# Two attention blocks on one core: block 1's tiles between block 0's scores, row maxima in two single PSUM banks, values of two steps together

## The chip, the cores and the metric

The kernel runs on one core of a Trainium2 chip. The metric is the device time of one execution in microseconds (us). Engines are named as in the profile: PE is TensorE's matmuls, PEld its weight loads, DVE is VectorE, ACT is ScalarE, POOL is GpSimd, SP is SyncE, whose queue issues all the transfers.

## The reference

Two blocks follow each other on x of shape (16, 128, 32, 32), float32, so on 16 images with 128 channels and N = 1024 positions each.

```python
# block 0: group norm (32 groups), 4 heads of 32 channels
_x = _group_norm(x, gn_scale, gn_bias)
q, k, v = (_lin_ch(_x, W, b).reshape(B, HEADS, dh, H, W) ...)
scores = jnp.einsum('bhdxy,bhdij->bhxyij', q, k) / sqrt(C)
weights = jax.nn.softmax(scores.reshape(B, HEADS, H, W, H * W), axis=-1)
h = jnp.einsum('bhxyij,bhdij->bhdxy', weights, v).reshape(B, C, H, W)
x = (x + _lin_ch(h, Wp, bp)) / sqrt(2.0)
# block 1: group norm (8 groups), one head of 128 channels
qkv = jnp.einsum('bnc,oc->bno', h_flat, qkv_w) + qkv_b
attn = jax.nn.softmax(jnp.einsum('bnc,bmc->bnm', q, k) / sqrt(C), axis=-1)
out = jnp.einsum('bnc,oc->bno', jnp.einsum('bnm,bmc->bnc', attn, v), proj_w) + proj_b
return out.transpose(0, 2, 1).reshape(B, C, H, W) + x
```

## The kernel before, in words

**Block 0.** For an image the group norm is applied on ScalarE (`norm`, L530), then q, k and v are projected in fp32 (`work`, L812). q and k are split into an fp32r high part (ScalarE, `high`, L540) and an fp32r low part (VectorE, `low`, L653). SP stacks the parts three deep on the partitions (`stack`, L339), so that one fp32r matmul over 97 rows makes a score; row 97 holds the negative row maximum, so exp needs no bias. Scores come transposed, keys on the partitions: a score is a matmul of 512 columns (queries of one half) for one head and one tile of 128 keys. An image has 16 steps (2 halves x 8 key tiles), each with 4 scores, one a head. ScalarE takes each through exp (`exp`, L483) into a slot of `probs`, a ring of 5 blocks; `pv` (L880) multiplies the four heads of a step with v in fp32, 32 columns a head, accumulating over 8 steps in the bank `acc`; GpSimd (`add`, L451) sums the exponentials into `sum0`, two instructions of 128x1024 for a step except the first of a half, 28 an image. At the end of the image TensorE sums over the keys (`sums`), SP sends the sums through `compact`, VectorE takes the reciprocals, SP spreads them through DRAM (`spread_reciprocals`, L385), VectorE scales `mix` (`scale`, L711), and the projection and the residual (`proj`, L853, `residual`, L716) give block 1's input.

The row maxima come earlier and from other matmuls: `masked` holds a copy of q's high part for each head with the other heads' channels zero. 64 matmuls of 128x512 an image (L822) go two by two into one of two pairs of PSUM banks, and one reduce of 128x1024 on VectorE takes each pair (`maxima`, L664). `gather` (L673), a transpose and `shift` (L684) bring the negative maxima into the stack.

**Block 1.** For one image there are 8 query tiles. A tile's scores are 6 fp32r matmuls of 512 columns (`score1`, L914 to L916) into two banks. VectorE reduces 128x1024 (`max1`, L724), ScalarE takes exp with a row sum (`exp1`, L507), TensorE transposes (`turn`, L919), ScalarE evicts (`evict`, L514), TensorE multiplies with v in fp32 (`pv1`, L925, 16 records a tile), ScalarE scales by the reciprocal of the row sum (`oevict`, L521), and after four tiles `out` transposes back and VectorE adds the residual.

**Order of the work.** It is written out by hand. An image's period has two stages: in x (64 gaps) TensorE issues a score of block 0 in each gap, in y (32 gaps) the eight tiles of block 1 of the image before it. Every engine issues in order; tables of pieces (`X_PIECES`, `Y_PIECES` and others) say for each piece in which gap TensorE, ScalarE and VectorE do their part of it. The maxima of the next image stand in gaps of both stages (`MAX_X`, `MAX_Y`). Eight PSUM banks: `acc` 1, `duo` 2, `lone` 1, two pairs of 2. Block 0's scores rotate over `duo` and `lone`, so score n waits for the exp of score n-3. The two pairs serve maxima, q, k, v, means, sums, projection, out; pair 1 and `duo` also serve block 1's tiles; the tiles' outputs go to `lone` and `acc`. In what order they are used is worked out by `pair_uses` (L124), and a piece waits until its pair's last user has given it back.

## Time and profile before

| | us |
|---|---|
| median of 3 runs | 1874.27 (1872.96 to 1874.69) |
| the profiled execution | 1874.44 |
| its span, first to last instruction | 1872.7 |
| PE, PEld busy | 1673.2 (89%), 1050.8 (56%) |
| DVE, ACT, POOL busy | 1057.7 (56%), 1024.9 (55%), 1086.2 (58%) |
| mean granted clock of TensorE | 0.971 |

Busy time of PE counts overlapping records. TensorE's pace is read from the starts of its groups. In the timeline a group is start, length, engine, line, what it writes and reads, shape and count; in brackets stands the idle time before it and what ended it.

### The profile page before, as it was taken

How to read it: one execution, taken by the hardware profiler on the slowest of the kernel's cores; microseconds unless marked ns; L12 is line 12 of the kernel's file. 1: busy time of each engine (PE TensorE's matmuls, PEld its weight loads, DVE VectorE, ACT ScalarE, POOL GpSimd, SP SyncE). 2: the span in 40 equal slices, each digit the busy share in tenths (PEclk: the TensorE clock that was granted, in tenths of full speed). 3: DMA queues.
4: the chain of work that ended last, by engine and by line, in shares of the span. 5: the costliest groups of instructions: out<-in, count | busy, mean ns of one | idle time of the engine just before them, and what ended most of it. 6: DMA issues, size and time to landing. Idle time of an engine off the chain costs nothing.

```text
span 1872.7 us, 24868 instructions
## 1 busy us (share of the span) xinstructions
PE 1673.2 (89%) x9304; PEld 1050.8 (56%) x9304; DVE 1057.7 (56%) x1254; ACT 1024.9 (55%) x1713; POOL 1086.2 (58%) x493
## 2 busy tenths in 40 slices
PE   5888898998989989898998989999898998998878
PEld 3434574745647465564745647475564746555367
DVE  5585646556554655646566554655645565563632
ACT  1535556564655656555564655656555564555644
POOL 1684828477382865828476382856828376493600
PEclk8889999999999999999999999999999999999889
DMA  5031210413122031310313122041311303131000
GB/s 139 24 79 24 66 52 9 96 30 85 41 45 64 18 91 35 79 47 13 84 29 91 35 56 54 17 96 30 79 47 25 73 29 80 35 68 36 1 18 18
DMA packets 52790, 95.41 MB, mean 51 GB/s; under 512 B 27328, under 2 KB 27968, under 8 KB 52672
## 3 DMA queue, kind: packets, MB, share of 16 engines
q1 hardware_dynamic: 52672, 93.83, 20.3%
q8 instruction: 75, 1.23, 0.3%
q14 instruction: 43, 0.35, 0.1%
HBM read 25.89 MB, written 8.65 MB: 18 GB/s over the span
## 4 chain that ended last, share of the span: by engine, by line
PE 45%; issue 27%; POOL 13%; DVE 9%; ACT 5%; DMA 1%; SPq 0%; ACTq 0%; POOLq 0%; DVEq 0%
POOL sum L459 13%; PE acc L939 7%; PE pair L822 7%; DVE halfmax L669 5%; PE lone L939 4%; PE pair L828 4%; PE acc L894 3%; PE duo L922 2%; PE duo L877 2%; ACT probs L498 2%; PE pair L922 2%; PE pair L832 2%; PE pair L850 2%; PE duo L914 1%; PE duo L915 1%
## 5 line engine op out<-in xcount | busy, mean ns | idle before, releaser
L459 POOL TENSOR_TENSOR sum<-sum,probs 128x1024 f32<-128x1024 f32 x437 | 1042.5, 2425 | 527.1 <-PE acc L894 525.0
L669 DVE TENSOR_REDUCE halfmax<-pair 128x2 f32<-128x1024 f32 x512 | 616.9, 1221 | 380.0 <-PE pair L822 378.0
L498 ACT ACTIVATE probs<-duo 128x512 f32<-128x512 f32 x608 | 347.2, 599 | 236.2 <-PE duo L877 198.9
L822 PE MATMUL pair<-k_hi,masked 128*128 128x512 f32 x1024 | 377.2, 452 | 84.4 <-DVE halfmax L669 56.6
L822 PEld LDWEIGHTS pair<-k_hi,masked 128*128 128x128 f32 x1024 | 172.1, 197 | 252.1 <-DVE halfmax L669 102.6
L877 PE MATMUL duo<-q_stack,k_stack 97*128 97x512 f32 x688 | 283.0, 445 | 24.8 <-ACT probs L498 20.5
L894 PE MATMUL acc<-probs,v 128*32 128x512 f32 x1792 | 241.3, 611 | 0.2 <-ACT probs L498 0.2
L498 ACT ACTIVATE probs<-lone 128x512 f32<-128x512 f32 x288 | 173.4, 602 | 101.7 <-PE lone L877 70.4
L877 PEld LDWEIGHTS duo<-q_stack,k_stack 97*128 97x128 f32 x688 | 128.6, 191 | 136.9 <-ACT probs L498 89.7
L939 PEld LDWEIGHTS acc<-v,turned 128*128 128x128 f32 x1280 | 158.9, 192 | 27.2 <-issue 18.8
L939 PE MATMUL acc<-v,turned 128*128 128x128 f32 x1280 | 165.7, 277 | 1.7 <-ACT mixed L527 1.7
L877 PE MATMUL lone<-q_stack,k_stack 97*128 97x512 f32 x336 | 143.7, 428 | 17.4 <-ACT probs L498 17.2
L518 ACT COPY turned<-duo 128x1024 f32<-128x1024 f32 x64 | 64.8, 1013 | 120.9 <-PE duo L922 120.9
L518 ACT COPY turned<-pair 128x1024 f32<-128x1024 f32 x64 | 64.7, 1011 | 117.9 <-PE pair L922 117.9
L443 POOL TENSOR_TENSOR gn<-gn,minus_half 128x1 f32<-128x1 f32 x32 | 18.6, 581 | 184.4 <-DVE gn L645 184.4
L661 DVE SCALAR_TENSOR_TENSOR q_lo<-pair,bq_scaled,q_hi 128x1024 fp32r<-128x1024 f32 x32 | 41.1, 1284 | 115.6 <-ACT q_hi L551 115.6
L877 PEld LDWEIGHTS lone<-q_stack,k_stack 97*128 97x128 f32 x336 | 63.9, 190 | 67.2 <-ACT probs L498 44.4
L726 DVE TENSOR_REDUCE negmax<-pair 128x1 f32<-128x1024 f32 x64 | 78.2, 1222 | 39.2 <-PE pair L916 39.1
L726 DVE TENSOR_REDUCE negmax<-duo 128x1 f32<-128x1024 f32 x64 | 78.2, 1223 | 39.0 <-PE duo L916 37.9
L939 PEld LDWEIGHTS lone<-v,turned 128*128 128x128 f32 x768 | 91.6, 192 | 7.4 <-issue 6.2
L939 PE MATMUL lone<-v,turned 128*128 128x128 f32 x768 | 93.5, 275 | 0.0
L894 PEld LDWEIGHTS acc<-probs,v 128*32 128x32 f32 x1792 | 35.6, 109 | 79.0 <-issue 53.4
(99 smaller groups left out, 2014.8 us busy)
## 6 DMA issues: line engine op xcount, KB each, us to landing
q_stack<-q_hi SPq DMA_DIRECT2D x128, 128.0 KB, 2.4
k_stack<-k_hi SPq DMA_DIRECT2D x128, 128.0 KB, 2.5
xin<-x_dram SPq DMA_DIRECT2D x16, 512.0 KB, 3.7
x<-x_dram SPq DMA_DIRECT2D x16, 512.0 KB, 3.5
masked<-q_hi SPq DMA_DIRECT2D x64, 128.0 KB, 2.4
q_stack<-q_lo SPq DMA_DIRECT2D x64, 128.0 KB, 2.5
k_stack<-k_lo SPq DMA_DIRECT2D x64, 128.0 KB, 2.5
rb<-recip_dram SPq DMA_DIRECT2D x64, 128.0 KB, 2.7
```

Source lines behind the costliest of these rows:

```text
L459: pool.tensor_tensor(total, total, probs[:, ring_slot(i, half, kt), 2 * two:2 * two + 2, :], ALU.add).then_inc(added[two], 1)
L498: act.activation(dst, score_bank(index), ACT.Exp).then_inc(exp_done, 1)
L518: act.copy(turned[:, t % 2, :, :].rearrange("p k n -> p (k n)"), score1_pair(t)[:, :]).then_inc(evicted, 1)
L661: dve.scalar_tensor_tensor(out=lo[:, :], in0=pairs[p][:, :], scalar=bias, in1=hi[:, :].bitcast(F32), op0=ALU.add, op1=ALU.subtract).then_i ...
L669: dve.tensor_reduce(halfmax[:, 2 * two:2 * two + 2, t, half], pairs[p][:, :].rearrange("p (h n) -> p h n", h=2), AX.X, ALU.max).then_inc(p ...
L726: dve.tensor_reduce(negmax[:, t:t + 1], score1_pair(t)[:, :], AX.X, ALU.max, negate=True).then_inc(negmax_done, 1)
L822: mm = pe.matmul(dst[:, halves(n)], masked[:, h, tile(t)], part[2][:, halves(half)], start=True, stop=True)
L828: mm = pe.matmul(dst[:, halves(half)], weight, xh[:, halves(half)], start=True, stop=True)
L877: pe.matmul(score_bank(index), ks[0:SPLIT + 1, h, tile(kt)], qs[0:SPLIT + 1, h, halves(half)], start=True, stop=True).then_inc(score_full, 1)
L894: mm = pe.matmul(acc[head(h), :], v0[:, i % 2, kt, head(h)], src, start=kt == 0, stop=kt == KT - 1, tile_position=(0, DH * h))
L922: mm = pe.transpose(score1_pair(t)[:, tile(kt)], probs1[:, t % 2, tile(kt)], identity)
L939: mm = pe.matmul(out_bank(t), turned[:, t % 2, kt, :], v1[:, kt, :], start=kt == 0, stop=kt == KT - 1)
```

## The change

There is one kind of round in place of the stages x and y: 64 gaps, in each a score of block 0. Block 1's tiles of the image before stand in it, one every 8 gaps from gap 38 of one round to gap 40 of the next. A tile uses the two banks of `scores1` alone, and one copy of `probs1` and of `turned` (in the closing round alone a second set lies in `scores` and `probs`, and tiles stand 4 gaps apart). Banks are now: `scores` 3 (block 0's scores rotate over them), `acc` 1, `scores1` 2, and two single banks for all that the pairs did and for the tiles' outputs (`pv1`). The maxima take a bank each: 64 matmuls and 64 reduces of 128x512 an image, from gap 23 of the round before to gap 10, 11 in 8 gaps, none in gaps 33 to 36 and 42. q, k, v, sums, reciprocals, scale, projection, residual, statistics of block 1 and shift go by halves of 512. `pv` of two steps is issued together in every eighth gap (10, 18, ...). The ring of `probs` has 3 blocks instead of 5. Queries are stacked by halves into three slots and keys into two, so an image has 36 stack transfers instead of 24 (the same bytes), two shift transfers, and twice the sums' and reciprocals' transfers with half the bytes. The last image's adds on VectorE are gone. The head has 32 single maxima of image 0, round 0 the other 32.

```diff
-RING = 5
+RING = 3
-MAX_X = (0, 4, 6, 13, 15, 20, 22, 24, 26, 28, 30, 32, 37, 39, 42, 44, 46, 50, 53, 55, 57, 59, 61, 63)
-MAX_Y = (0, 4, 6, 8, 10, 12, 14, 16)
...
+GAPS = 4 * STEPS
+MAXES = 2 * KT * HEADS
+TILE_GAPS, TILE_FIRST = 8, 38
+def tile_pieces(t, first):
+    return [("score1", (t, 0), 0, first, None, None), ("score1", (t, 1), 0, first + 1, None, None),
+            ("max1", t, 0, None, None, first + 1), ("exp1", t, 0, None, first + 3, None),
+            ("rinv", t, 0, None, None, first + 4), ("turn", t, 0, first + 5, first + 5, None),
+            ("pv1", t, 0, first + 10, first + 11, None)]
+BLOCK1 = [(p[0], p[1], -1) + p[3:] for t in range(KT) for p in tile_pieces(t, TILE_FIRST + TILE_GAPS * t)] + [
+    ("out", 0, -1, GAPS + 11, None, GAPS + 11), ("out", 1, -1, GAPS + 43, None, GAPS + 43)]
+VALUES = [("pv", n, 0, 8 * n + 10, None, None) for n in range(STEPS // 2)]
+MAX_PLACES = (1, 1, 2, 1, 2, 1, 1, 2)
+MAX_FROM = 23
+MAX_NOT = (33, 34, 35, 36, 42)
+MAX_GAPS = [g for g in range(MAX_FROM, 2 * GAPS) if g not in MAX_NOT
+            for _ in range(1 if g == MAX_NOT[0] - 1 else MAX_PLACES[(g - TILE_FIRST) % TILE_GAPS])][:MAXES]
+ALL_MAX = max_pieces(range(MAXES), MAX_GAPS, 1)
+EARLY_MAX = [p for n, p in enumerate(ALL_MAX) if n + 1 < MAXES and MAX_GAPS[n + 1] == MAX_GAPS[n]]
+LATE_MAX = [p for p in ALL_MAX if p not in EARLY_MAX]
+SHIFTS = [("gather", 0, 1, None, None, MAX_HALF), ("shift", 0, 1, MAX_HALF + 1, None, MAX_HALF + 1),
+          ("gather", 1, 1, None, None, MAX_ALL), ("shift", 1, 1, MAX_ALL + 1, None, MAX_ALL + 1)]
+NEXT0 = [
+    ("stats0", 0, 1, None, None, 3), ("mean0", 0, 1, 5, None, 5), ("var0", 0, 1, 7, None, 7),
+    ("affine0", 0, 1, None, None, 11), ("norm0", 0, 1, None, 12, None),
+    ("q0", 0, 1, 17, 17, 18), ("q0", 1, 1, 17, 17, 18), ("k0", 0, 1, 19, 19, 20), ("k0", 1, 1, 19, 19, 20),
+    ("v0", 0, 1, 21, 21, None), ("v0", 1, 1, 21, 21, None),
+]
+CHAIN = [
+    ("save", 0, 0, None, 35, None),
+    ("sums", 0, 0, 44, 44, None), ("recip", 0, 0, None, None, 48), ("scale", 0, 0, None, None, 55),
+    ("proj", 0, 0, 60, None, 60), ("stats1", 0, 0, None, None, 61),
+    ("save", 1, 0, None, GAPS + 3, None),
+    ("sums", 1, 0, GAPS + 6, GAPS + 6, None), ("recip", 1, 0, None, None, GAPS + 9),
+    ("scale", 1, 0, None, None, GAPS + 14), ("proj", 1, 0, GAPS + 15, None, GAPS + 15),
+    ("stats1", 1, 0, None, None, GAPS + 16), ("mean1", 0, 0, GAPS + 22, None, GAPS + 22),
+    ("var1", 0, 0, GAPS + 24, None, GAPS + 24), ("affine1", 0, 0, None, None, GAPS + 28),
+    ("norm1", 0, 0, None, GAPS + 29, None),
+    ("q1", 0, 0, GAPS + 33, GAPS + 33, GAPS + 34), ("q1", 1, 0, GAPS + 33, GAPS + 33, GAPS + 34),
+    ("k1", 0, 0, GAPS + 35, GAPS + 35, GAPS + 36), ("k1", 1, 0, GAPS + 35, GAPS + 35, GAPS + 36),
+    ("v1", 0, 0, GAPS + 42, GAPS + 42, None), ("v1", 1, 0, GAPS + 42, GAPS + 42, None),
+]
+ROUND = folded(EARLY_MAX + VALUES + BLOCK1 + CHAIN + NEXT0 + SHIFTS + LATE_MAX)
...
+def bank_uses(images):
+    back = {VE: dict(all_pieces(VE, images)), SC: dict(all_pieces(SC, images))}
+    uses, counts, last, free = {}, [[0, 0], [0, 0]], [None, None], [(-1, 0), (-1, 0)]
+    for piece, _ in all_pieces(PE, images):
+        if piece[0] in BANKED:
+            b = 0 if free[0] <= free[1] else 1
+            uses[piece] = (b, sum(counts[b]), counts[b][0], counts[b][1], last[b])
+            last[b] = BANKED[piece[0]]
+            free[b] = (back[last[b]][piece], len(uses))
+            counts[b][0 if last[b] == VE else 1] += 1
...
+        scores = ps("scores", [C, 3, HALF])
         acc = ps("acc", [C, HALF])
-        duo = ps("duo", [C, N])
-        lone = ps("lone", [C, HALF])
-        pairs = [None, ps("pair1", [C, N])]
-        pairs[0] = ps("pair0", [C, N])
+        scores1 = ps("scores1", [C, N])
+        banks = [ps(f"bank{b}", [C, HALF]) for b in range(2)]
...
-                    for n, h in enumerate((2 * two, 2 * two + 1)):
-                        mm = pe.matmul(dst[:, halves(n)], masked[:, h, tile(t)], part[2][:, halves(half)], start=True,
-                                       stop=True)
+                    mm = pe.matmul(dst[:, :], masked[:, h, tile(t)], part[2][:, halves(half)], start=True, stop=True)
...
-                dve.tensor_reduce(halfmax[:, 2 * two:2 * two + 2, t, half],
-                                  pairs[p][:, :].rearrange("p (h n) -> p h n", h=2), AX.X,
-                                  ALU.max).then_inc(pair_free[p][VE], 1)
+                dve.tensor_reduce(halfmax[:, h, t, half:half + 1], banks[p][:, :], AX.X,
+                                  ALU.max).then_inc(bank_free[p][VE], 1)
...
+                        if name == "pv":
+                            pv(img, 2 * arg)
+                            pv(img, 2 * arg + 1)
```

An entry of a table names the piece, its argument, the image as an offset from the round's, and the gaps of PE, ACT and DVE. Within a gap the score comes first, then the pieces in the order of `ROUND`: early maxima, values, block 1, chain, next image, shifts, late maxima. `folded` moves entries from gap 64 on into the next round. `bank_uses` gives each piece the bank whose user gives it back first by the gaps of the tables.

## Rows read from the trace of the kernel before

**Rows 1.** The page's head and its busy times, whole execution.

```profile
span 1872.7 us, 24868 instructions
...
PE 1673.2 (89%) x9304; PEld 1050.8 (56%) x9304; DVE 1057.7 (56%) x1254; ACT 1024.9 (55%) x1713; POOL 1086.2 (58%) x493
```

**Rows 2.** Busy time by stage (length, busy by engine, PEclk, DMA share, GB/s).

```profile
0.00:55.90 55.90, 30.68 (x73) 15.36 (x73) 28.87 (x47) 5.76 (x5) 8.56 (x10) 0.77 0.44 117
55.90:149.40 93.50, 84.03 (x358) 41.07 (x358) 65.24 (x65) 44.43 (x74) 67.02 (x30) 0.90 0.24 57
149.40:1704.60 1555.20, 1420.48 (x8065) 899.57 (x8062) 893.12 (x1066) 889.36 (x1490) 960.13 (x433) 0.99 0.21 52
1704.60:1872.70 168.10, 138.03 (x815) 94.81 (x814) 70.50 (x76) 85.33 (x144) 50.50 (x20) 0.93 0.06 18
```

**Rows 3.** Timeline of TensorE, 700 to 745 us.

```profile
700.61 1.95 PE L939 MATMUL lone<-v,turned 128*128 128x128 f32 x16
702.40 0.60 PE L859 MATMUL pair<-consts,mixed 128*128 128x128 f32 x4
...
703.07 0.39 PE L915 MATMUL pair<-k_lo,q_hi 128*128 128x512 f32 x1
703.30 0.39 PE L916 MATMUL pair<-k_hi,q_lo 128*128 128x512 f32 x1
...
704.23 1.03 PE L922 MATMUL duo<-consts,probs 128*128 128x128 f32 x8
705.10 1.06 PE L939 MATMUL acc<-v,turned 128*128 128x128 f32 x8
706.09 1.92 PE L850 MATMUL pair<-sum,ones 128*32 128x512 f32 x16
707.94 1.16 PE L939 MATMUL acc<-v,turned 128*128 128x128 f32 x8
...
741.30 1.98 PE L828 MATMUL pair<-xh,wq_scaled 128*128 128x512 f32 x4
...
743.45 1.06 PE L894 MATMUL acc<-probs,v 128*32 128x512 f32 x8
744.44 0.50 PE L877 MATMUL lone<-q_stack,k_stack 97*128 97x512 f32 x1
744.78 1.88 PE L828 MATMUL pair<-xh,wts 128*128 128x512 f32 x4
```

**Rows 4.** Timeline, 727 to 735 us: reduces on VectorE and maxima around them.

```profile
727.25 1.23 DVE L669 TENSOR_REDUCE halfmax<-pair 128x2 f32<-128x1024 f32 x1 [1.88 <-PE pair L822]
728.39 1.22 DVE L721 TENSOR_TENSOR x<-pair,x 128x1024 f32<-128x1024 f32 x1
...
732.54 1.23 DVE L669 TENSOR_REDUCE halfmax<-pair 128x2 f32<-128x1024 f32 x1 [0.28 <-PE pair L822]
...
733.82 0.73 PE L822 MATMUL pair<-k_hi,masked 128*128 128x512 f32 x2 [0.63 <-DVE halfmax L669]
...
734.59 1.23 DVE L669 TENSOR_REDUCE halfmax<-pair 128x2 f32<-128x1024 f32 x1 [0.39 <-PE pair L822]
```

**Rows 5.** Groups by line and shape (count, busy us, mean ns, idle before); last row: min/median/max.

```profile
L669 DVE TENSOR_REDUCE halfmax<-pair 128x2 f32<-128x1024 f32 x512 | 616.9, 1221 | 380.0 <-PE pair L822 378.0
...
L726 DVE TENSOR_REDUCE negmax<-duo 128x1 f32<-128x1024 f32 x64 | 78.2, 1223 | 39.0 <-PE duo L916 37.9
...
L511 ACT ACTIVATE probs<-duo,negmax 128x1024 f32<-128x1024 f32 x64 | 71.6, 1118 | 4.5 <-DVE negmax L726 4.5
...
L661 DVE SCALAR_TENSOR_TENSOR k_lo<-pair,vecs,k_hi 128x1024 fp32r<-128x1024 f32 x32 | 41.0, 1280 | 46.2 <-ACT k_hi L551 46.2
...
L738 DVE SCALAR_TENSOR_TENSOR x<-pair,proj_bias,x 128x512 f32<-128x512 f32 x32 | 23.8, 745 | 64.5 <-PE pair L859 64.5
...
L714 DVE TENSOR_TENSOR mix<-mix,rb x16: 1225/2770/3056, 161.2 to 1785.0; 128x1024 f32<-128x1024 f32 x16
```

**Rows 6.** Groups of one image's period, 819.5 to 931.6 us.

```profile
L459 POOL TENSOR_TENSOR sum<-sum,probs 128x1024 f32<-128x1024 f32 x28 | 66.5, 2412 | 33.1 <-PE acc L894 33.1
```

**Rows 7.** Timeline of VectorE, 714 to 723 us: reciprocals and scale of one image.

```profile
714.36 0.35 DVE L709 RECIPROCAL compact<-compact 128x32 f32<-128x32 f32 x1 [1.84 <-DMA compact<-rb]
...
722.08 1.50 DVE L714 TENSOR_TENSOR mix<-mix,rb 128x1024 f32<-128x1024 f32 x1 [3.16 <-DMA rb<-recip_dram]
```

More of the change, by code:

```diff
@@ new lines, with rounds_of, pieces_of @@
+LAST_GAPS = LAST_AT[KT - 1, -1] + 12
+PE, SC, VE = 3, 4, 5
+BANKED = {"max": VE, "q0": VE, "k0": VE, "q1": VE, "k1": VE, "v0": SC, "v1": SC, "mean0": VE, "var0": VE, "mean1": VE,
+          "var1": VE, "shift": VE, "sums": SC, "proj": VE, "out": VE, "pv1": SC}
+def rounds_of(images):
+    return [("head", 0, HEAD_GAPS)] + [("round", i, GAPS if i < images else LAST_GAPS) for i in range(images + 1)]
+def pieces_of(kind, i, engine, gap, images):
+    table = HEAD if kind == "head" else ROUND_FIRST if i == 0 else ROUND_LAST if i == images else ROUND
+    return [(p[0], p[1], i + p[2]) for p in table if p[engine] == gap and 0 <= i + p[2] < images]
@@ new lines, in all_pieces @@
+def all_pieces(engine, images):
+    out, before = [], 0
+    for kind, i, gaps in rounds_of(images):
+        out += [(piece, before + gap) for gap in range(gaps) for piece in pieces_of(kind, i, engine, gap, images)]
+        before += gaps
+    return out
+def bank_uses(images):
[8 more added lines that the diff above has]
+            counts[b][0 if last[b] == VE else 1] += 1
@@ new lines, in row_sums @@
+            def row_sums(i, half):
+                piece = ("sums", half, i)
+                p = bank_of(piece)
+                act.wait_ge(bank_full[p], filled(piece))
+                if i:
+                    act.wait_ge(scaled, 2 * i + half - 1)
+                act.copy(rb[:, halves(half)], banks[p][:, :]).then_inc(bank_free[p][SC], 1)
+            act.wait_ge(prep_ve, PREP_VE)
+            for kind, i, gaps in rounds_of(images):
+                for gap in range(gaps):
+                    if kind == "round" and has0(i):
+                        exp(i, gap)
+                    for name, arg, img in pieces_of(kind, i, SC, gap, images):
+                        if name == "turn":
+                            evict(img, arg)
+                        elif name == "pv1":
+                            oevict(img, arg)
+                        elif name == "exp1":
+                            exp1(img, arg)
+                        elif name == "save":
+                            save(img, arg)
+                        elif name in ("norm0", "norm1"):
+                            norm(int(name[-1]), img)
+                        elif name in ("q0", "q1", "k0", "k1"):
+                            high(int(name[-1]), "qk".index(name[0]), arg, img)
+                        elif name in ("v0", "v1"):
+                            value(int(name[-1]), arg, img)
+                        elif name == "sums":
+                            row_sums(img, arg)
@@ L807, in take @@
-                if after_tiles and p == 1:
-                    pe.wait_ge(evicted, after_tiles)
-                return pairs[p], pair_full[p]
-            def work(piece, tiles):
-                name, arg, i = piece
-                dst, full = take(piece, tiles)
+                    pe.wait_ge(bank_free[p][last], by_ve if last == VE else by_sc)
+                dst = banks[p]
                 b = int(name[-1]) if name[-1] in "01" else 0
                 if name == "max":
-                    t, half, two = arg // 4, arg // 2 % 2, arg % 2
+                    t, half, h = arg // 8, arg // 4 % 2, arg % 4
```

910 lines of the change are left out of this document (386 added, 524 removed), and 12 rows, old and new, of tables (HEAD, HEAD_PIECES, X_PIECES, Y_LAST_PIECES).

## The prediction

> **What bounds the kernel now.** I read the page's head first, then busy time by stage, then TensorE's timeline, then the other engines' rows. TensorE is busy 89% of the span, no other engine over 58% [rows 1]; ahead of the first score stand 55.9 us, then 93.5 us for image 0's scores, 1555.2 us for fourteen like rounds (111.1 each, clock 0.99) and 168.1 us of tail [rows 2]. TensorE's rows are pipelined and overlap, so I count from start to start [rows 3]: a 512-column fp32r matmul 0.23 (703.07 to 703.30); a tile's eight transposes 0.87 (704.23 to 705.10); its sixteen value records 1.79 (700.61 to 702.40); values of one step of block 0 0.99, and the score behind them 0.34 instead of 0.23 (743.45, 744.44, 744.78), so each change to or from fp32 with 32 columns costs 0.1; two groups of row sums together 1.85 (706.09 to 707.94), so the second of two such groups costs only 0.86. A q with one score is 2.15 (741.30 to 743.45), so 1.72 for q itself.
>
> With these, an image of before needs: 64 scores, 64 maxima and 48 tile scores, 176 x 0.232 = 40.8; turns 8 x 0.87 = 7.0; tile values 8 x 1.79 = 14.3; block 0's values 16 x 1.2 = 19.2; q and k 6.9, v 3.6, projection 1.7, sums 2.0, out, means, shift 2.1. Sum 97.6 against 111.1: some 13.5 us per round are waits of TensorE. The change has to lower those, or the round gets no shorter.
>
> **The change, part by part.**
> *Values of two steps together:* one entry and exit saved per pair and the overlap of 1.85 against 2 x 0.99: 0.99+0.86+0.2 = 2.05 instead of 2.4, eight pairs: -2.8. Bound from the other side: nothing saved. I take -2.8, from the sums row.
> *Halves of q, k, v, projection, out:* same matmuls. Sums by halves 2 x 1.2 instead of 2.0: +0.4; a second shift +0.2. New need of TensorE: 95.4.
> *Single banks for the maxima:* 64 reduces of 512 in place of 32 of 1024. The trace has none. Lower bound half of 1.22, 0.61; by the shape that exists both ways (low parts, 1.28 for 1024, 0.745 for 512 [rows 5]) 512 elements save 0.53: 0.69, which I take; upper bound the 0.745 itself. VectorE then has about 70 us of work in a round (64 x 0.69, 8 x 1.22, 8 x 0.745, and 10 of small ones), so it is no bound. But the loop through one bank is: a matmul of 0.40 ends and the reduce starts 0.04 later, the matmul that waited starts 0.05 after the reduce [rows 4]; so a bank is back 0.43+0.69+0.05 = 1.17 after its matmul started. Before, a pair took 0.23+0.43+1.22+0.05 = 1.93 but carried two matmuls, and ScalarE's output tiles stood in other banks. Now pv1, out, sums, q, k, v share the two.
> *Tiles between scores:* every 8 gaps hold 8 scores, a tile (6 scores, turn, values), a value pair, and 11 maxima. Time 0 at the first gap, from the rows above:
> gaps 1, 2: score, three tile scores, maximum 1 (0.93); score, three tile scores (last at 1.86), maximum 2 at 2.09. VectorE's list has the tile's reduce of 1024 before maximum 2: it runs 2.29 to 3.51 [rows 5], maximum 2's reduce 3.43 to 4.12 (back to back an op starts 0.09 before the end of the last, as at 728.39 [rows 4]).
> gap 3: score, maximum 3, and the last tile's values take maximum 2's bank: could start 2.78, start at 4.17. **Wait 1.39.** They end 5.87; maximum 4.
> gap 4: score, maximum 5 in the bank of maximum 4: 6.42 becomes 7.04. **Wait 0.62.**
> gap 5: score, maximum 6, value pair, maximum 7; gap 6: turn, maximum 8 (exp of the tile, 1.12 [rows 5], is ready); gap 7: maximum 9; gap 8: maxima 10, 11: **waits 0.16 and 0.37.**
> So 2.5 us per full cycle. I went through all 64 gaps of a round so, by the order of the lists. Gaps 38 to 45: 1.39+0.62, sums behind out 0.5, maxima behind the sums copy 0.35: 2.9. 46 to 53: 2.0, and shift between maxima 1.3: 3.3. 54 to 61: 2.0, scale ahead of a maximum 1.1, maxima behind the projection 0.8: 3.9. 62 to 5: 2.3, statistics (1.5 on VectorE) ahead of a maximum and mean between two maxima 1.8: 4.1. 6 to 13: 1.15+0.62, and the second shift, which TensorE reaches 1.6 before out's add, affine and gather are through: 3.4. 14 to 22: 0.6. 23 to 29: 3.0. 30 to 37: q behind a maximum 0.6, maxima behind k's low parts 1.2: 1.8. Sum of waits 23.0; round 95.4+23.0 = **118.4 us** against 111.1.
> *Scale:* its row is 1.2 at least, 2.77 in the median [rows 5]; for halves I took 0.7 to 1.5. The Trainium skill ("SBUF — State Buffer", section "SBUF: two separate sides") has VectorE with two SBUF inputs and GpSimd lock each other out for a whole instruction; the spread of that row agrees. By it a half would still wait out an add: 0.9 more per round, 1981 in all.
> *Queues and ring:* GpSimd's adds are 28 x 2.41 = 66.5 per image [rows 6]; ring 3 needs an add within some 5 gaps (9 us) and gets it in 4.8 to 7: nothing in full rounds. Sync's queue issues 36 stack transfers instead of 24, all behind gap 18 and due a round later: nothing, with the rest of the round as cover; without it one more set of 12, some 8 us. The reciprocals: recip stands 8.3 us behind the sums' start, scale 7.4 behind recip [rows 7]; the new places leave 7.5 and 7 or more, so at most 1 us, taken as 0.
> *The ends:* head: no statistics of image 1 (-2), one shift transfer for four (-2), single reduces (+2): 54. Round 0: the adds bound it: they start at gap 10 (17 us), the second half starts at gap 42 (52), and the exp of gap 60 needs eight adds of it (19): 71, and 4 to its end: 75. Round 1 lacks four tiles (21) and 3 of waits: 94.4. Rounds 2 to 15: 14 x 118.4 = 1657.6. Tail: sums of the last half at 7, reciprocals to 20, projection, norm, q, k to 38, eight tiles x 4.05 = 32, last values, out, store 14: 84 to 86, I take 85.
> Sum 54+75+94.4+1657.6+85 = 1966; what lies around the span is 1874.4-1872.7 = 1.7 (the profiled execution is 0.2 over the median shown): **1968**. It turns on the round: 1.7+190+15 x P for a round P (the span of before is met at P = 112.2).
>
> **Rivals.**
> (a) *TensorE's waits are fewer* (faster). Place: the irregular stretches. A wait makes the next one shorter, and of the 23 us I may count neighbours twice; if only the regular waits of the six tile cycles stay, 13.7 minus a little, P = 108: 1812. It decides from waits under 16.8 per round. For it: before has only 13.5. Against: each is a row's loop with nothing between; the cycle was followed through. 0.13.
> (b) *Even*, waits of 16 to 17.5: 1874. 0.04.
> (c) *The pairing saves nothing* (the change doesn't do that part): P = 121.2: 2010. 0.08.
> (d) *The clock.* It stood at 0.99 with 13 us of waits and at 0.90 to 0.93 in the sparser ends [rows 2]. If the rounds went to 0.92, TensorE's need is 95.4/0.93: P about 125, 2065. 0.05. The Trainium skill ("TensorE: Matmul & The Clock Gate", section "A second HAM failure mode: psum-queue depth-cycling") tells of small idles between groups that cycle through banks and bring the clock down; the 0.99 beside 13 us of waits per round speaks against; by the rule it would be (d)'s 2065.
> Forecast: 0.70.
>
> **Numbers.** The reduce's bounds move about a dozen waits a round each by its error once or twice: 0.61 gives P = 116, 0.745 gives 120: 1930 to 1990; with my error in the irregular waits, 3 us a round each way, 1900 to 2010. To hold 8 in 10 the range takes in (b), part of (a) and (c): 1860 to 2020. Faster by over 0.2% (about what a measurement here can tell from no change) 0.13, within 0.04, slower 0.83.
>
> **What would show it.** Score 0 of one round to the next 118 apart; reduces of 128x512 at 0.69; tile values waiting 1.4 for a maximum's reduce, that behind the tile's own reduce; the second of two maxima in one bank 0.6 late; no GpSimd wait within full rounds; value pairs 1.85 long; granted clock over 0.97. Wrong: a round under 112, or waits of TensorE mostly for exps or adds.

## The result and the profile after

| | before | after |
|---|---|---|
| median | 1874.5 us (4 runs) | 2067.2 us (4 runs, 2065.3 to 2068.1) |
| ratio to before | | 1.103, interval 1.101 to 1.105 |
| span of the profiled execution | 1872.7 | 2063.2 |

The change makes the kernel 10% slower. The sign was forecast, with 0.83; the size was not: 1968 was said, 1860 to 2020 as the range, and the measured time lies 47 us above its upper end.

The page's head, busy times and chain of the kernel after:

```profile
span 2063.2 us, 26122 instructions
...
PE 1733.4 (84%) x9319; PEld 1070.5 (52%) x9319; DVE 1128.9 (55%) x1897; ACT 1061.1 (51%) x1825; POOL 1103.3 (53%) x504
...
PE 65%; DVE 24%; issue 5%; ACT 3%; DMA 2%; SPq 1%; POOL 0%; ACTq 0%; DVEq 0%; POOLq 0%
PE bank L912 12%; DVE halfmax L708 12%; PE bank L879 12%; PE acc L838 11%; PE scores L825 7%; PE scores L863 5%; DVE negmax L750 4%; PE bank L887 3%; PE scores L855 3%; PE scores L857 3%; PE bank L883 3%; PE scores L856 3%; DVE mix L737 2%; PE bank L901 2%; DVE k_lo L699 2%
```

TensorE's share falls from 89% [rows 1] to 84%, and no other engine is fuller: nobody is the bound. The chain says what is: it goes to and fro between TensorE and VectorE. VectorE has 24% of it with 55% busy, and half of that is the reduces of the maxima (L708).

By stage (head, round 0, round 1, thirteen rounds, round 15, tail; columns as in [rows 2]):

```profile
0.00:58.30 58.30, 33.35 (x68) 15.26 (x68) 31.64 (x56) 6.44 (x8) 11.42 (x9) 0.79 0.41 112
58.30:149.00 90.70, 80.05 (x297) 35.85 (x297) 62.13 (x100) 42.68 (x73) 64.92 (x29) 0.86 0.21 50
149.00:255.80 106.80, 89.23 (x416) 47.32 (x415) 64.27 (x108) 54.36 (x93) 68.62 (x33) 0.92 0.19 45
255.80:1883.90 1628.10, 1378.00 (x7568) 860.48 (x7567) 910.07 (x1535) 859.73 (x1482) 887.68 (x404) 0.98 0.19 47
1883.90:1971.60 87.70, 80.49 (x503) 52.06 (x502) 32.91 (x56) 59.27 (x106) 60.09 (x27) 1.00 0.06 19
1971.60:2063.20 91.60, 72.26 (x475) 59.56 (x473) 27.87 (x46) 38.60 (x64) 10.58 (x6) 0.93 0.05 15
```

The thirteen full rounds take 1628.1/13 = 125.2 us each where 118.4 was said. TensorE has no matmul under way for 250.1 of the 1628.1 us, 19.2 a round. The waits view of the whole execution (us in total, times, longest):

```profile
PEld bank L879 <- DVE halfmax L708: 221.5, 330, 4.3
...
PEld bank L912 <- DVE halfmax L708: 150.8, 82, 3.9
...
PE bank L912 <- DVE halfmax L708: 115.3, 69, 3.5
...
PE bank L879 <- DVE halfmax L708: 82.8, 166, 4.0
```

Two things wait for a maximum's reduce: the next maximum's matmul (L879) and the values of block 1's tile (L912). Weight loads and matmuls overlap, so the first and last number are not to be added; of the matmuls alone it is 115.3 + 82.8 = 198.1 us. The groups by form give the reduce and the scale:

```profile
L708 DVE TENSOR_REDUCE halfmax<-bank 128x1 f32<-128x512 f32 x1024 | 679.1, 686 | 446.4 <-PE bank L879 444.1
...
L737 DVE TENSOR_TENSOR mix<-mix,rb 128x512 f32<-128x512 f32 x32 | 57.0, 1780 | 4.6 <-DMA rb<-recip_dram 4.5
```

The reduce of 128x512 takes 0.686 us, as said (0.69), 56% of the 1.221 of the double one [rows 5]. The scale of a half takes 1.78 in the mean, where 0.7 to 1.5 was counted.

**One tile, as it repeats.** Timeline of the kernel after, a tile's last scores, its reduce and its neighbour's values:

```profile
1131.22 0.39 PE L857 MATMUL scores<-k_hi,q_lo 128*128 128x512 f32 x1
...
1131.45 0.39 PE L879 MATMUL bank<-k_hi,masked 128*128 128x512 f32 x1
...
1131.65 1.23 DVE L750 TENSOR_REDUCE negmax<-scores 128x1 f32<-128x1024 f32 x1 [0.21 <-PE scores L857]
...
1132.79 1.28 DVE L708 TENSOR_REDUCE halfmax<-bank 128x1 f32<-128x512 f32 x2
...
1133.53 2.05 PE L912 MATMUL bank<-v,turned 128*128 128x128 f32 x16 [1.22 <-DVE halfmax L708]
...
1135.34 0.48 PE L879 MATMUL bank<-k_hi,masked 128*128 128x512 f32 x1
...
1135.85 0.69 DVE L708 TENSOR_REDUCE halfmax<-bank 128x1 f32<-128x512 f32 x1 [1.78 <-PE bank L879]
...
1136.60 0.50 PE L879 MATMUL bank<-k_hi,masked 128*128 128x512 f32 x1 [0.55 <-DVE halfmax L708]
```

The maximum of 1131.45 could be reduced at 1131.88. VectorE's list has the tile's reduce of 1024 first (1131.65 to 1132.88), so its bank is back at 1133.48, and the values of the tile before, which take that bank, stand at the head of TensorE's queue with everything behind them. That is the wait forecast at 1.39; the gaps of the steady rounds give 1.49. The next pair of maxima in one bank was put at 0.62 and is 0.82: the fp32r matmul right behind fp32 groups lasts 0.48 to 0.50 instead of 0.40, so the reduce behind it starts later.

**Where the scale stands.** The same kernel, one gap of each round:

```profile
1111.81 4.71 POOL L509 TENSOR_TENSOR sum<-sum,probs 128x1024 f32<-128x1024 f32 x2
...
1113.39 0.39 PE L879 MATMUL bank<-k_hi,masked 128*128 128x512 f32 x1
...
1113.59 1.22 DVE L750 TENSOR_REDUCE negmax<-scores 128x1 f32<-128x1024 f32 x1 [0.24 <-PE scores L857]
...
1114.73 2.33 DVE L737 TENSOR_TENSOR mix<-mix,rb 128x512 f32<-128x512 f32 x1
1116.99 1.27 DVE L708 TENSOR_REDUCE halfmax<-bank 128x1 f32<-128x512 f32 x2
1117.72 2.58 PEld L912 LDWEIGHTS bank<-v,turned 128*128 128x128 f32 x16 [3.91 <-DVE halfmax L708]
1117.72 2.67 PE L912 MATMUL bank<-v,turned 128*128 128x128 f32 x15 [3.47 <-DVE halfmax L708]
...
1120.25 0.77 PE L879 MATMUL bank<-k_hi,masked 128*128 128x512 f32 x1
```

And by stretch, the wait and what follows it (columns as in [rows 2], the granted clock third from the end):

```profile
1115.00:1117.70 2.70, 0.00 (x0) 0.00 (x0) 2.70 (x3) 0.00 (x0) 1.52 (x1) 1.00 0.00 0
...
1118.80:1122.20 3.40, 3.04 (x12) 2.32 (x12) 0.69 (x1) 0.71 (x2) 0.04 (x1) 0.51 0.00 0
```

In this gap the tile's reduce and then the scale stand ahead of the maximum's reduce. The scale lasts 2.33 us: it ends at 1117.06, half a microsecond after GpSimd's add (1111.81 + 4.71 = 1116.52). Where no add runs the same multiply takes 0.69 (the last one of this trace, at 1993.26). It takes 0.67 where it comes just at the change from one add to the next, and then the add behind it lasts 2.89 instead of 2.4 (e1's timeline below, at 1087.16). So most of the 2.33 is waiting for the add. The Trainium skill ("SBUF — State Buffer", section "SBUF: two separate sides") calls the port pair shared by VectorE with two SBUF inputs and GpSimd "an exclusive lock, not a bandwidth split"; this trace agrees, 2.33 beside an add against 0.69 without.

**What the long wait does to TensorE's clock.** Gap 56 has a median of 7.56 us, 5.07 more than its 2.49 in e8, the shortest of all runs. Not all of that is waiting. After the 3.47 us without a matmul TensorE's granted clock falls from 1.00 to 0.5, its level of 1.2 GHz, and the values and the maximum behind them take 2.88 us (all sixteen records) and 0.77 instead of 2.05 and 0.48. It does so in gap 56 of eleven of the thirteen full rounds (7.56 us in the mean); in the two without a fall the gap takes 6.18 and 6.22. So the wait itself is 3.7 us, and 1.4 are TensorE working at half its clock. Gap 6 shows the same: 3.79 us in the mean of nine rounds with a fall there, 2.36 in the four without. Ahead of it stand only short waits (in this round 0.73 and 0.30 us, behind maxima's reduces, at 1017.32 and 1018.60). Together the falls leave TensorE at 0.5 for 5.3 us of a full round and cost about 2.1 us of it (my sum of the gaps: (9 x 1.43 + 11 x 1.36)/13).

### The profile page after: what moved, and what is told of

Read it like the earlier page. It is cut to its first block, busy times and chain, and to the rows that moved or that the text cites. A ratio compares the mean times of both kernels' runs of the same rounds, so it can differ in the third digit from the quotient of the medians.

```text
span 2063.2 us, 26122 instructions
## 1 busy us (share of the span) xinstructions
PE 1733.4 (84%) x9319; PEld 1070.5 (52%) x9319; DVE 1128.9 (55%) x1897; ACT 1061.1 (51%) x1825; POOL 1103.3 (53%) x504
## 4 chain that ended last, share of the span: by engine, by line
PE 65%; DVE 24%; issue 5%; ACT 3%; DMA 2%; SPq 1%; POOL 0%; ACTq 0%; DVEq 0%; POOLq 0%
PE bank L912 12%; DVE halfmax L708 12%; PE bank L879 12%; PE acc L838 11%; PE scores L825 7%; PE scores L863 5%; DVE negmax L750 4%; PE bank L887 3%; PE scores L855 3%; PE scores L857 3%; PE bank L883 3%; PE scores L856 3%; DVE mix L737 2%; PE bank L901 2%; DVE k_lo L699 2%
## 5 line engine op out<-in xcount | busy, mean ns | idle before, releaser
L708 DVE TENSOR_REDUCE halfmax<-bank 128x1 f32<-128x512 f32 x1024 | 679.1, 686 | 446.4 <-PE bank L879 444.1
L544 ACT ACTIVATE probs<-scores 128x512 f32<-128x512 f32 x896 | 523.4, 601 | 649.7 <-PE scores L825 647.2
L879 PE MATMUL bank<-k_hi,masked 128*128 128x512 f32 x1024 | 486.4, 480 | 119.1 <-DVE halfmax L708 82.8
L825 PE MATMUL scores<-q_stack,k_stack 97*128 97x512 f32 x1024 | 445.1, 445 | 2.2 <-DMA q_stack<-neg 2.2
L879 PEld LDWEIGHTS bank<-k_hi,masked 128*128 128x128 f32 x1024 | 199.6, 195 | 386.5 <-DVE halfmax L708 221.5
L912 PE MATMUL bank<-v,turned 128*128 128x128 f32 x1952 | 261.5, 290 | 116.6 <-DVE halfmax L708 115.3
L912 PEld LDWEIGHTS bank<-v,turned 128*128 128x128 f32 x1952 | 244.3, 202 | 156.5 <-DVE halfmax L708 150.8
L825 PEld LDWEIGHTS scores<-q_stack,k_stack 97*128 97x128 f32 x1024 | 196.9, 194 | 71.3 <-issue 28.7
L750 DVE TENSOR_REDUCE negmax<-scores 128x1 f32<-128x1024 f32 x128 | 156.7, 1225 | 77.3 <-PE scores L857 77.3
L557 ACT ACTIVATE probs<-scores,negmax 128x1024 f32<-128x1024 f32 x128 | 143.0, 1117 | 3.4 <-DVE negmax L750 3.4
L855 PE MATMUL scores<-k_hi,q_hi 128*128 128x512 f32 x256 | 105.2, 411 | 4.4 <-DVE k_lo L699 3.2
```

Of the source, the lines that this page charges most:

```text
L544: act.activation(dst, score_bank(i, index), ACT.Exp).then_inc(exp_done, 1)
L708: dve.tensor_reduce(halfmax[:, h, t, half:half + 1], banks[p][:, :], AX.X, ALU.max).then_inc(bank_free[p][VE], 1)
L750: dve.tensor_reduce(negmax[:, t:t + 1], score1_pair(j, t), AX.X, ALU.max, negate=True).then_inc(negmax_done, 1)
L825: pe.matmul(score_bank(i, index), ks[0:SPLIT + 1, i % 2, h, tile(kt)], qs[0:SPLIT + 1, q_half(i, half), h, :], start=True, stop=True).then ...
L855: pe.matmul(dst, q_hi[:, tile(t)], k_hi[:, halves(half)], start=True, stop=False)
L879: mm = pe.matmul(dst[:, :], masked[:, h, tile(t)], part[2][:, halves(half)], start=True, stop=True)
```

## The experiments

Theory A, from the two timelines: a round's TensorE work is what was counted (95.4), and the rest are waits of TensorE at the head of its queue for a reduce that stands late in VectorE's list; the two single banks are what ties the two queues together. Rival B: the round is longer for a reason that the gaps don't show one by one (adds, exps, the smaller ring, a slower TensorE). Rival C: it is the other parts of the change, the pairs of values or the single kind of round.

Times and ratios below are medians of 4 runs (e5 and e6 of 2, e12 of 10) against the kernel before on the same chip. A full round is the mean over rounds 2 to 14, from score 0 of one to score 0 of the next; its "waits" are each gap's median length less the TensorE work counted for it, 95.4 a round. So they hold what TensorE loses at the lower clock too, and they can't confirm the count.

| run | us | ratio [interval] | full round | waits in it | at clock 0.5 |
|---|---|---|---|---|---|
| after | 2067.2 | 1.103 [1.101, 1.105] | 125.2 | 29.8 | 5.3 |
| e1 tile's reduce last | 1941.5 | 1.037 [1.035, 1.039] | 116.3 | 20.5 | 0.3 |
| e2 first scale on GpSimd | 2004.7 | 1.070 [1.069, 1.072] | 121.7 | 26 | 2.1 |
| e3 values one by one | 2077.4 | 1.109 [1.107, 1.110] | 125.9 | | 3.2 |
| e4 three banks | 1805.6 | 0.963 [0.962, 0.965] | 107.4 | 12.4 | 1.8 |
| e8 e1 + e2 + e4 | 1745.6 | 0.933 [0.931, 0.934] | 103.6 | 7.8 | 0.0 |
| e10 e8, pieces a gap later | 1750.0 | 0.934 [0.933, 0.936] | 103.6 | 7.9 | 0.0 |
| e11 e8, values one by one | 1768.9 | 0.944 [0.942, 0.946] | 105.3 | 9.7, or 6.9 of a work of 98.2 | 0.0 |

The last column is how long TensorE's granted clock stands at 0.5 in a full round, in us. In the kernel before it is 2.4.

**e1: the order of VectorE's list alone.**

```diff
-                    for name, arg, img in pieces_of(kind, i, VE, gap, images):
+                    for name, arg, img in sorted(pieces_of(kind, i, VE, gap, images), key=lambda p: p[0] == "max1"):
```

> Edit of the changed kernel: within a gap VectorE does the tile's own reduce of 1024 last, behind the maxima of that gap. Theory A (TensorE waits because the two single banks come back only through VectorE's queue): the tile values' wait of 1.49 us, six times a round, shrinks to about 0.5; 6 us a round less, round 125.2 to 119, total about 1980 us. Theory B (tiles between scores cost by themselves, through ScalarE or the changes of type): no change, 2067 us.

Measured: 1941.5. The same place of a tile in e1's timeline, and a scale further on:

```profile
1060.70 0.39 PE L879 MATMUL bank<-k_hi,masked 128*128 128x512 f32 x1
...
1061.13 0.69 DVE L708 TENSOR_REDUCE halfmax<-bank 128x1 f32<-128x512 f32 x1 [0.44 <-PE bank L879]
...
1061.73 1.22 DVE L750 TENSOR_REDUCE negmax<-scores 128x1 f32<-128x1024 f32 x1
1061.87 1.86 PEld L912 LDWEIGHTS bank<-v,turned 128*128 128x128 f32 x16 [0.75 <-DVE halfmax L708]
1061.87 2.05 PE L912 MATMUL bank<-v,turned 128*128 128x128 f32 x16 [0.32 <-DVE halfmax L708]
...
1087.16 0.67 DVE L737 TENSOR_TENSOR mix<-mix,rb 128x512 f32<-128x512 f32 x1
```

The maximum is reduced at once, the values wait 0.32 instead of 1.22 (0.58 instead of 1.49 by the gaps), and in gap 56 it is 1.44 instead of 5.07. Nothing else was changed, no instruction added or removed: 126 us of the 193 that the change costs come from the place of one reduce among its neighbours. A full round is 8.9 shorter, not the 6 expected, because two things follow from the shorter wait. The scale in gap 55 takes 1.50 us instead of 2.33 (it starts 0.9 later in GpSimd's add, and again ends 0.55 after it), and the clock, which fell 20 times in the thirteen full rounds, falls once, some 2 us of the 8.9. So the slower TensorE that B names is there, but as a consequence of these waits; for the rest B is out for this part.

**e2: the first half's scale on GpSimd**, behind its add of that gap instead of beside it.

```diff
+                        pool.wait_ge(rb_loaded, 16 * HEADS * (2 * i + 1))
+                        pool.wait_ge(saved, 2 * i + 1)
+                        pool.tensor_tensor(mix[:, halves(0)], mix[:, halves(0)], rb[:, halves(0)],
+                                           ALU.mult).then_inc(scaled, 1)
...
-                            scale(arg, img)
+                            if arg:
+                                scale(arg, img)
```

> Edit of the changed kernel: the scale of an image's first half is done on GpSimd, behind its add 21 and the forming of x1, instead of on VectorE between two reduces in gap 55. Theory A: the wait of 5.07 us in gap 56 falls to the 1.49 us of the other tiles, 3.6 us a round less, total about 2015 us. Theory B: 2067 us. If GpSimd's place is too late, the projection in gap 60 waits and eats the gain.

Measured: 2004.7; gap 56 waits 1.49, as a regular tile. GpSimd does it in 1.30 us (20.8 us for 16, group L527) and TensorE waits 0.3 us for it in the whole run. So one instruction of a half, at its place, costs the kernel 62 us, 3.5 a round, where the sum had held 1.1 for it. About 2.2 of the 3.5 are its wait (3.7 in gap 56 without a fall, less the 1.49 of a regular tile), most of the rest is the lower clock behind it, which no longer comes in gap 56.

**e3: pairs of values undone.**

```diff
-VALUES = [("pv", n, 0, 8 * n + 10, None, None) for n in range(STEPS // 2)]
+VALUES = [("pv", n, 0, 4 * n + 6, None, None) for n in range(STEPS)]
...
-                            pv(img, 2 * arg)
-                            pv(img, 2 * arg + 1)
+                            pv(img, arg)
```

> Edit of the changed kernel: block 0's values one step at a time again, every four gaps, three gaps behind the step's last score, as the pair stands behind its second step. Pairing as computed (2.05 us for two instead of 2.4): 2.8 us a round more, total about 2109 us. Rival (a pair of 2 us blocks TensorE and costs more than it saves): total under 2067 us. If the extra 0.35 us lie in waits for VectorE's banks anyway: about 2067 to 2085 us.

Measured: 2077.4, so 10 us for all the pairs, 0.7 a round (0.9 by the gaps' medians) in place of 2.8. C is out for the pairs: they are not what costs, and they hardly help here. That what a pair saves of TensorE's work is spent in the next wait for a bank fits, but no run shows it by itself. The single kind of round is no cause either: e5 and e8 below keep it.

**e4: three single banks, two banks of scores** in place of two and three, so that score n waits for the exp of score n-2.

```diff
-        scores = ps("scores", [C, 3, HALF])
+        scores = ps("scores", [C, 2, HALF])
...
-        banks = [ps(f"bank{b}", [C, HALF]) for b in range(2)]
+        banks = [ps(f"bank{b}", [C, HALF]) for b in range(3)]
...
-            b = 0 if free[0] <= free[1] else 1
+            b = min(range(3), key=lambda k: free[k])
```

> Edit of the changed kernel: three single banks for maxima and the rest, two instead of three for block 0's scores; nothing else. Theory A: of the 29.8 us of waits in a round the tile values', the second maximum's and the double maxima's go; 8 to 12 us stay (scale, statistics, q and k), round 104 to 108, total 1770 to 1830 us. Rival (TensorE then waits for exps, with two score banks): over 1950 us. Theory B: 2067 us or more.

Measured: 1805.6, inside theory A's range, 262 us less, and faster than before. Waits fall from 29.8 to 12.4 a round. The bank that the scores lose is hardly missed: in the thirteen full rounds a score's weight load waits 23.6 us in all for an exp, 1.8 a round, and no wait of its matmul for one is among the larger. Its waits view has the first line of the one above at 123.9, and none of the tile's values behind a reduce among its larger ones:

```profile
PEld bank L879 <- DVE halfmax L708: 123.9, 228, 5.9
...
PE bank L879 <- DVE halfmax L708: 49.2, 51, 5.4
```

**e5 and e6: the maxima left out**, in the kernel after and in the one before. Both compute only those of the row maxima that the order of the waits needs (5 of 64 in e5, 3 of 32 double ones in e6) and start `halfmax` at zero; everything else is done.

```diff
-    return [(p[0], p[1], i + p[2]) for p in table if p[engine] == gap and 0 <= i + p[2] < images]
+    return [(p[0], p[1], i + p[2]) for p in table if p[engine] == gap and 0 <= i + p[2] < images
+            and (p[0] != "max" or p[1] in (0, 30, 31, 62, 63))]
```

> Edit of the changed kernel: of the 64 maxima of an image only numbers 0, 30, 31, 62 and 63 are made, the others' places hold zero, so the shift of the scores is another; all else stays. Theory A (the waits are those behind the maxima's reduces): the need falls by 59 x 0.23 = 13.7 to 81.8 us a round and the waits from 29.8 to 4 or 6 us, round 86 to 88, total 1490 to 1530 us. Theory B (tiles between scores cost by themselves): the waits stay near 20 us, total over 1700 us.

> Edit of the kernel before: of the 32 pairs of maxima only numbers 0, 15 and 31 are made, the others' places hold zero; all else stays. It gives what the maxima cost in the old order: their need is 29 x 0.46 = 13.3 us an image; if they also bear half of its 13.5 us of waits, about 91 us an image, total 1540 us; if they bear none, 98 us, 1655 us. Both theories agree here; the difference to the changed kernel without maxima is what the new order is worth by itself (theory A: the new order is the shorter one by 30 to 60 us, theory B: the longer one).

Measured: e5 1551.6 (0.829), rounds of 90.0; e6 1702.0 (0.909), 101.4 from image to image. By stage, e5's full rounds and e6's images:

```profile
203.30:1373.90 1170.60, 1089.56 (x6801) 710.86 (x6800) 425.16 (x767) 843.43 (x1483) 890.39 (x404) 1.00 0.26 65
```

```profile
122.20:1440.00 1317.80, 1204.99 (x6759) 714.87 (x6756) 385.91 (x622) 817.75 (x1387) 889.24 (x403) 0.95 0.23 57
```

Both missed what was expected, and together they say more than either: without maxima the new order is 150 us **shorter** than the old one, with them 193 longer. The maxima cost the old order 1874 - 1702 = 172 us and the new one 2067 - 1552 = 515, which is 32 an image. Of these 59 x 0.232 = 13.7 are the matmuls; the other 18.5 are waits that only the maxima bring, with the lower clock behind some of them. Taking them out of the old order saves less than their own matmuls (172/16 = 10.8 an image, where 29 x 0.46 = 13.3 are matmuls). Its waits view shows one reason, more waits for exps:

```profile
PEld duo L879 <- ACT probs L499: 184.5, 254, 2.6
```

against 89.7 us for that pair with the maxima there. A second reason is the clock, 0.95 in e6's stage line and 1.00 in e5's: TensorE stands at 0.5 for 10.2 us of every image of e6, 2.4 in the kernel before. Half of the difference, up to 3.9 us an image or some 60 us in all, can be the lower clock; the two reasons are not separated, and up to that much of the 150 us between e5 and e6 can be the clock's. My reading is that in the old order the maxima filled holes between exps, and that in the new one, with the tiles spread out, few such holes are left (8 us a round in e5), so that the maxima make their own.

**e7: pairs of values in the old order.**

```diff
-                            if (n, h) == (2, 0) or (n >= 2 and h == 2):
-                                pv(i, n - 1 - (h == 0))
+                            if n >= 2 and n % 2 == 0 and h == 2:
+                                pv(i, n - 2)
+                                pv(i, n - 1)
...
+                        pv(i, STEPS - 2)
                         pv(i, STEPS - 1)
```

> Edit of the kernel before: block 0's values two steps together, all else as it was; this part of the change alone. If TensorE's need sets the old stages: 16 x 2.8 = 45 us less, 1829 us. If what TensorE saves is lost in waits for exps and adds: 1850 to 1874 us. Over 1874 us if the pair of 2 us starves ScalarE.

Measured: 1933.2 (1.033 [1.030, 1.035]): the edit that was to shorten TensorE's work costs 59 us, 4.1 an image. From score 0 the scores run with those of before within 1.9 us up to the middle of the image; by score 43 they are 3.3 us late, and the first add behind `rstd` starts at 60.1 instead of 57.4. TensorE's clock falls to 0.5 26 times in thirteen images instead of 9. In the kernel before an image with a fall takes 112.1 and one without 110.7, so by that price the clock can be some 1.9 of the 4.1.

**e9: the same with the first and last step of each half alone**, six pairs an image.

> Edit: the kernel before, values of two steps issued together as in e7, but the first step of each half (0 and 8) and the last of each half (7, 15) alone and where they stood; six pairs an image instead of eight. In e7 the first add of the second half, which waits for the values of step 8, started 60.1 us after score 0 instead of 57.4, and the image took 116 instead of 112.1 (e7: 1933). If that late value is what made e7 slower: the add of the second half is back at 57.4, and the six pairs save at most 6 x 0.35 = 2.1 us an image: 1840 to 1875. If two steps together stall ScalarE or the score banks by themselves: six eighths of e7's loss stay, 1905 to 1925.

Measured: 1918.4 (1.024 [1.023, 1.026]), add at 60.0. A late first value is not the cause. The timeline shows another:

```profile
664.25 0.73 PE L822 MATMUL pair<-k_hi,masked 128*128 128x512 f32 x2
...
665.16 1.92 PE L894 MATMUL acc<-probs,v 128*32 128x512 f32 x16
...
667.01 0.38 PE L838 MATMUL pair<-gn,consts 128*128 128x1 f32 x2
...
667.43 0.16 DVE L645 TENSOR_SCALAR gn<-pair 128x1 f32<-128x1 f32 x1 [1.18 <-PE pair L838]
...
667.67 0.55 POOL L443 TENSOR_TENSOR gn<-gn,minus_half 128x1 f32<-128x1 f32 x1 [7.59 <-DVE gn L645]
...
668.19 4.70 POOL L459 TENSOR_TENSOR sum<-sum,probs 128x1024 f32<-128x1024 f32 x2
...
670.73 0.60 ACT L498 ACTIVATE probs<-lone 128x512 f32<-128x512 f32 x1 [2.35 <-POOL sum L459]
...
671.37 0.50 PE L877 MATMUL lone<-q_stack,k_stack 97*128 97x512 f32 x1 [2.00 <-ACT probs L498]
```

An image takes 114.0 against 111.0 before. The only one of the thirteen in which the clock doesn't fall takes 113.2, against 110.7 for those of the kernel before, so 2.5 of the 3.0 are there at the full clock.

Read from below: a score waits for an exp, the exp for a slot of the ring, the slot for GpSimd's add, the add for `rstd` ahead of it in GpSimd's list (idle 7.59 us), `rstd` for VectorE, VectorE for a small matmul of TensorE, and that stands behind the pair of values. A loop through four engines, and the pair lengthens it.

**e12: `rstd` four adds later in GpSimd's list**, else e9.

```diff
-                    if n == 14 and has0(i + 2):
+                    if n == 18 and has0(i + 2):
```

> Edit: e9 (before with six value pairs an image, 1918 us) and GpSimd computes the next image's rstd behind add 18 of an image instead of add 14. Seen in e9's trace: GpSimd's add 15 stands behind rstd, rstd behind VectorE's var0, var0 behind a matmul that TensorE issues after a value pair of 1.92 us; the adds start 2.6 us later than before (60.0 instead of 57.4 after score 0), an exp waits 2.35 us for one of them, and a score 2.00 for that exp. If this detour of GpSimd is where the pairs lose their time, the 2.6 to 3.3 us an image that are lost behind gap 44 come back and more: 1865 to 1885. If the time goes where TensorE's long pair leaves ScalarE without scores, rstd changes little: 1905 to 1920.

Measured: 1872.7 (1.000 [0.999, 1.001], 10 runs), inside the first theory's range: 46 us from one instruction moved. Its images take 110.6 without a fall of the clock and 112.1 with one, as those of before, so 2.6 of what came back is at the full clock. The add behind add 14 starts at 51.8 instead of 60.0, and the waits view has

```profile
ACT probs L498 <- POOL sum L459: 7.3, 2, 7.1
```

against 70.5 in e9 and 65.8 before. It is not the whole story of the pairs. ScalarE's waits for scores (the lines `ACT probs` behind `duo` and `lone`) are 269.5 us before, 314.5 in e9 and 337.6 in e12, so six pairs in the old order give nothing even then. Whether the later `rstd` without any pairs beats the kernel before was not tried.

**e8: the three edits together** (e1, e2, e4).

> The changed kernel with three single banks, the tile's reduce last in its gap, and the first half's scale on GpSimd. With three banks 12.4 us of waits are left in a round of 107.9, 4.4 of them in gaps 56 and 58 around the scale. Theory A: these go, the tile's order adds 0 to 0.5, round 104, total 1745 to 1760 us. If GpSimd's place for the scale is too late: the projection's gap takes the wait over, 1790 to 1806 us.

Measured: 1745.6, inside the first theory's range and 6.7% less than before: the best version here. Its full rounds (13 of them), and its chain:

```profile
223.90:1570.80 1346.90, 1296.45 (x7567) 851.07 (x7567) 870.67 (x1522) 856.97 (x1482) 902.82 (x417) 1.00 0.23 57
```

```profile
PE 75%; DVE 13%; issue 4%; ACT 4%; DMA 2%; SPq 1%; POOL 1%; ACTq 0%; DVEq 0%; POOLq 0%
```

**e10: e8 with `mean0`, `var0` and the second shift one gap later**, where its largest waits were left.

```diff
-    ... ("mean0", 0, 1, 5, None, 5), ("var0", 0, 1, 7, None, 7),
+    ... ("mean0", 0, 1, 6, None, 6), ("var0", 0, 1, 8, None, 8),
...
-          ("gather", 1, 1, None, None, MAX_ALL), ("shift", 1, 1, MAX_ALL + 1, None, MAX_ALL + 1)]
+          ("gather", 1, 1, None, None, MAX_ALL), ("shift", 1, 1, MAX_ALL + 2, None, MAX_ALL + 2)]
```

> Edit: e8 (1746) with mean0 and var0 one gap later (6, 8) and the second shift one gap later (13), since the two largest waits left in its round stand there (gap 12 1.29 us, gap 5 1.14). If each wait is only a static order by which TensorE reaches a piece before VectorE has got to it, both fall to 0.3 or so: 1.5 to 1.8 us a round, 1718 to 1728. If what a wait gives back is mostly taken by the next (the banks are the bound), 0 to 0.5 a round: 1738 to 1750.

Measured: 1750.0, no gain, as the second theory had it. Gap 5's wait of 1.14 became 0.63, 0.34 and 0.53 in gaps 5, 6 and 8; gap 12's 1.29 became 1.18 in gap 13. A likely reason is that TensorE reaches a moved piece just as early relative to its neighbours on VectorE, since both lists moved together.

**e11: e8 with the values one by one**, e3's edit.

> Edit: e8 (1746) with the values of one step in every fourth gap instead of two in every eighth. In e3, with 30 us of waits in a round, undoing the pairs cost 0.9 us a round, where I had counted 2.8 of TensorE's need. If the 2.8 were right and e3's waits swallowed the rest, then here, with 8 us of waits, it costs 2 to 2.8 a round: 1776 to 1791. If the pairs save less of TensorE than I counted, about 0.9 a round: 1755 to 1765.

Measured: 1768.9, between the two ranges and 23 us more than e8. A round takes 105.3 against 103.6 (105.2 against 103.2 by the gaps' medians). So the pairs are worth 1.7 to 1.9 of the 2.8 where few waits are left, and 0.7 to 0.9 where many are.

## Why the prediction was right and wrong

Its span of 1966 against the 2063.2 measured, by its own terms: head 54 became 58.3 (+4), round 0 75 became 90.7 (+16), round 1 94.4 became 106.8 (+12), thirteen full rounds +89, round 15 118.4 became 87.7 (-31), the tail 85 became 91.6 (+7). Sum +97.

**What held.** The single-bank reduce is 0.686 for 0.69. TensorE's need, 95.4, was counted from single rows and is not measured by itself; it agrees with e8, whose 103.6 us a round leave 8.2 above it, and with e5 (90.0, its need 81.8). The mechanism is the one named: values of a tile behind a maximum's reduce behind the tile's own reduce (1.49 for 1.39), the second maximum in one bank (0.82 for 0.62). The ring of three, the 36 transfers and the reciprocals cost nothing in full rounds: what waits there is named by the waits view, and it is mostly the reduces.

**The step that failed: the waits of a round, 23.0, where its gaps leave 29.8 above the count.** About 27.2 of these are waits. The other 2.6 are TensorE at the lower clock in a usual round, for which the sum held nothing; rival (d) had the clock at a chance of 0.05. By stretch, said and measured: gaps 38 to 45 2.9, 3.3; 46 to 53 3.3, 3.7; **54 to 61 3.9, 6.8**; 62 to 5 4.1, 4.2; 6 to 13 3.4, 4.8; 14 to 22 0.6, 0.7; 23 to 29 3.0, 4.0; 30 to 37 1.8, 2.3. None came out smaller. The clock's falls stand in two of them: 1.4 of the 6.8 in gap 56, and 1.3 of the 4.8 in gap 6, nearly all that 6 to 13 has above what was said.
- The largest piece is "0.7 to 1.5" for the scale of a half. The row had shown 2.77 in the median for the whole [rows 5], and the sum took the lower half of it; measured 2.33 beside an add, which made gap 56 5.07 (3.7 of waiting, 1.4 of lower clock) instead of the cycle's 1.39 and what the scale was given. The lock of the Trainium skill ("SBUF — State Buffer", section "SBUF: two separate sides"), which the prediction had kept apart at 0.9 a round, held; the scale's whole price was 3.5 (e2). It stands, with the tile's reduce, ahead of the reduce that frees a bank, and the clock falls behind so long a wait.
- The loop through one bank was counted with the plain matmul of 0.40. Behind fp32 groups it is 0.50, so 1.27 in place of 1.17, six or more times a round.
- Irregular places with several small VectorE pieces between two maxima (gaps 5, 24, 29, 37) were each 0.3 to 0.6 short.

**Round 0.** "The adds bound it: 71, and 4 to its end" gave 75. Without maxima that is right (e5: 73.7). With them the banks bind this round too: 90.7, and 81.7 with three banks (e4). The first half's scale is as large a part of it: it takes 4.01 us in this round (at 132.72, across two adds), and with it on GpSimd the round is 83.4 (e2). Round 1 likewise, 77.0 in e5 against 106.8.

**Round 15** was counted as a full round in "rounds 2 to 15: 14 x 118.4". It has no next image, so no maxima, q, k, v of one. That error of 31 us went the other way and hid a quarter of the rest; with its measured length the same sum gives 1937.

**The rivals.** (a), waits that shrink one another: no stretch came out below its count. The two in which long waits follow each other (54 to 61, 6 to 13) came out furthest above, and the clock's falls are in these two: without them 6 to 13 is as counted, and 54 to 61 is 1.5 above, 1.1 of it the scale's (2.2 for 1.1). (c), pairing saves nothing, is nearly what e3 shows (0.7 to 0.9 of 2.8), though for another reason than that the edit does nothing: e11 gets 1.7 to 1.9 from it. (d), the clock at 0.92, did not come: it is 0.98 in the full rounds, 120 us of a round at the 2.4 GHz level and 5.3 at 1.2. It cost 2.1 us a round and not 7, so the time of (d), 2065, was met by chance, for the most part by other means. The Trainium skill ("TensorE: Matmul & The Clock Gate", section "A second HAM failure mode: psum-queue depth-cycling") has small idles between groups that cycle through banks bring the clock down again and again. This case's rows agree in part: 20 falls in the thirteen full rounds of the changed kernel, in gaps 6 and 56 alone, and one in e1, whose rounds still have 20.5 us of waits.

**What stays open.** Whether `rstd` four adds later helps the kernel before by itself; what the 8 us of waits that are left in e8 could still give; of round 0's 16 us, how much is the clock (0.86 in after, 0.90 in e8); why the clock falls in gap 6 in nine rounds and not in the four others; and how much of what e6, e7 and e9 show is the clock.

## What to carry to other kernels

When single buffers go round between an engine that fills them and one that empties them, look at the emptier's list: a long instruction just ahead of the one that frees a buffer costs its whole length at the head of the filler's queue, and moving it behind costs nothing (126 us here for one sort of a list). Count what a third buffer gives (262 us here) before counting what fewer or shorter instructions give (10 to 23 us for the pairs), and take the third from the ring that isn't waited for. Price an instruction that shares a port with a busy neighbour by the rows in which it met that neighbour, and ask who stands behind it. A gap that is too long isn't all waiting: look at the granted clock behind the wait before pricing it.
